# A Mamba block with SwiGLU on one core: GpSimd holds the product of beat 47, not of beat 48, behind the scan of beat 45

## The reference

```python
x_in, res = split(x @ W_in)                     # 512 + 512 columns
u = silu(causal_conv4(x_in))
dt, Bm, Cm = split(u @ W_x, [16, 32])
delta = softplus(dt @ W_dt + b_dt)
# 512 channels, 16 states each, a recurrence over the rows of a sequence:
h = exp(delta * A) * h + (delta * u) * Bm       # the scan
y = sum_over_states(h * Cm) + u * D
x = layernorm(x + (y * silu(res)) @ W_out)
x = layernorm(x + (silu(x @ Wg.T) * (x @ Wu.T)) @ Wd.T)
```

## Time and profile before

| | us |
|---|---|
| median of 3 runs | 1825.21 (1825.11 to 1825.59) |
| the profiled execution | 1827.21 |
| its span, first to last instruction | 1825.4 |
| PE busy | 1683.4 (92%) |
| DVE busy | 1711.8 (94%) |
| ACT busy | 1599.6 (88%) |
| POOL busy | 1646.8 (90%) |
| mean granted TensorE clock | 0.993 of full speed |

### The profile page before, as it was taken

The page is one execution under the profiler, slowest core; times in us unless marked ns, Lnnn a source line. Parts: engine busy times, 40 slices in busy tenths (PEclk is TensorE's granted clock), DMA queues, the critical chain, the costliest instruction groups (busy, mean ns, idle before and its releaser), DMA issues. The chain is left out here.

```text
span 1825.4 us, 32557 instructions
## 1 busy us (share of the span) xinstructions
PE 1683.4 (92%) x10128; PEld 1272.4 (70%) x10128; DVE 1711.8 (94%) x1958; ACT 1599.6 (88%) x2769; POOL 1646.8 (90%) x1629
## 2 busy tenths in 40 slices
PE   8879898999989899898999989899898999989788
PEld 3546686776767677676776767677676776767667
DVE  4999999999999999999999999999999999999994
ACT  4897989899898998989899898998989899898864
POOL 3999899998999999899998989999899998989970
PEclk9999999999999999999999999999999999999999
DMA  7323123222222323222232222323222232311010
GB/s 241 116 70 116 48 82 105 82 105 82 105 77 86 108 90 116 67 85 104 82 113 74 106 80 83 115 83 116 71 82 104 82 116 71 115 61 59 36 47 24
DMA packets 82108, 164.57 MB, mean 90 GB/s; under 512 B 10369, under 2 KB 28033, under 8 KB 81938
## 3 DMA queue, kind: packets, MB, share of 16 engines
q1 hardware_dynamic: 80498, 160.90, 25.6%
q10 hardware_dynamic: 1440, 1.58, 0.3%
HBM read 87.47 MB, written 8.91 MB: 53 GB/s over the span
## 5 line engine op out<-in xcount | busy, mean ns | idle before, releaser
L1236 POOL TENSOR_TENSOR dbu<-du,brep 128x512 f32<-128x512 f32 x1024 | 1315.1, 1314 | 120.6 <-DVE h L1431 97.0
L1431 DVE TENSOR_TENSOR_SCAN h<-da,carry,dbu 128x512 f32<-128x512 f32 x928 | 1151.6, 1271 | 54.7 <-ACT da L1093 42.5
L1093 ACT ACTIVATE da<-delta,a_s 128x512 f32<-128x512 f32 x928 | 641.6, 700 | 38.7 <-DVE h L1431 36.0
L1102 ACT ACTIVATE gt<-ht_upper,ct 128x512 f32<-128x512 f32 x512 | 353.3, 690 | 121.7 <-PE ht_upper L736 119.9
L736 PEld LDWEIGHTS ht_upper<-ident,h 128*128 128x128 f32 x2048 | 247.9, 141 | 215.8 <-issue 127.9
L736 PE MATMUL ht_upper<-ident,h 128*128 128x128 f32 x2048 | 311.7, 275 | 75.6 <-ACT gt L1102 46.3
L1443 DVE SCALAR_TENSOR_TENSOR acc<-ht_lower,ct,acc 128x512 f32<-128x512 f32 x480 | 349.3, 728 | 12.6 <-PE ht_lower L736 10.9
L736 PE MATMUL ht_lower<-ident,h 128*128 128x128 f32 x2048 | 312.9, 276 | 19.2 <-DVE acc L1443 16.7
L761 PE MATMUL y_upper<-ident,gt 128*128 128x128 f32 x2048 | 311.1, 275 | 0.0
L736 PEld LDWEIGHTS ht_lower<-ident,h 128*128 128x128 f32 x2048 | 240.2, 142 | 83.1 <-DVE h L1431 39.4
L761 PEld LDWEIGHTS y_upper<-ident,gt 128*128 128x128 f32 x2048 | 243.5, 142 | 56.0 <-issue 37.3
(11 more groups left out here) (189 smaller groups left out, 1909.6 us busy)
## 6 DMA issues: line engine op xcount, KB each, us to landing
brep<-b_rows SPq DMA_DIRECT2D x127, 512.0 KB, 3.7
xs<-xin SPq DMA_DIRECT2D x242, 256.0 KB, 2.5
xr<-x SPq DMA_DIRECT2D x16, 512.0 KB, 3.9
xt_s<-x_t SPq DMA_DIRECT2D x15, 512.0 KB, 3.8
out<-xr SPq DMA_DIRECT2D x15, 512.0 KB, 2.9
win_s<-w_in SPq DMA_DIRECT2D x2, 512.0 KB, 5.2
h<-xin SPq DMA_DIRECT2D x4, 256.0 KB, 4.3
h<-xin ACTq DMA_DIRECT2D x4, 256.0 KB, 4.7
```

The costliest lines, as they stand in the source:

```text
L1093: nc.scalar.activation(dst[:, :], delta[:, par, m, :], ACT.Exp, scale=a_s[:, m, n:n + 1])\
L1102: nc.scalar.activation(gt[:, (n * UPPER + k) % GT, :], ht_upper[:, :], ACT.Copy, scale=ct[:, par, k, n:n + 1])\
L1236: nc.gpsimd.tensor_tensor(dbu[:, beat % DBU, :], du[:, par, m, :], brep[:, n // PIECE % 2, n % PIECE, :], ALU.mult).then_inc(dbu_ready, 1)
L1431: nc.vector.tensor_tensor_scan(h[:, n % 2, m, 0:T], da[beat % 2][:, :] if slot is None else da_ahead[:, slot, :], dbu[:, beat % DBU, :], c ...
```

## The change

One number changes. HELD was {35: 33, 48: 45} and becomes {35: 33, 47: 45}. Product 47 now waits for scan 45 instead of scan 43. Product 48 waits for scan 44, as its buffer asks, which product 47's wait already includes. No instruction is added, removed or moved on any engine.

```diff
 AHEAD = 3
 DBU = 4
-HOLD = (4, 5)
+HOLD = (4, 4)
```

## The result

The changed kernel takes 1833.97 us (median of 5 runs, 1832.17 to 1835.08) against 1825.21 (1824.31 to 1825.59): a ratio of 1.0046, 95% interval 1.0031 to 1.0061. It is slower, by 8.8 us in the medians. The direction and the mechanism were forecast; the forecast was +5.8. The time lies above the 1829.0 to 1833.5 that the forecast had for itself, and inside the range of 1827.0 to 1834.0 by 0.03 us only.

What follows compares the result with a forecast made beforehand. GpSimd's gapless run from product 48 to the next chunk's product 0 was taken as the bound; +0.45 us in 11 middle chunks (4.95) plus the end chunks gave +5.8, 1825.2 to 1831.0 us, range 1827.0 to 1834.0.

Steps and rivals of the forecast that it cites:

- The bound: GpSimd, without idle time from product 48 to the next chunk's product 0, sets the loop of 109.14 us.
- The rival that VectorE sets the chunk: Each of 15 chunks would end 0.84 us earlier, -12.6, giving 1812.6 us; chance 0.07.
- The rival that scan 44 stays long: Scan 44 still held by something else, product 48 only delayed, 1.29 us in some 14 chunks: 1843 us; chance 0.04.
- The absorbed case: Delay mostly absorbed: product 48 only +0.22 us later per chunk, +2.4 in all, 1827.6 us; chance 0.14.
- The gain at scan 45: In a middle chunk scan 45 starts 0.84 us earlier, scan 44 being unstretched and up1's product waiting for its matmuls.
- The bound of 1.07: Largest gain at scan 45, 1.07 us, if the modelled end of up1's matmuls is too late; product 48 then +0.22.
- The delay: Product 47 and the copy precede product 48 after scan 45: 1.43 us against 0.15, so product 48 comes 1.29 later.
- The sum per loop: At product 48 in a middle chunk: -0.84 + 1.29 = +0.45 us, bounds +0.22 and +0.6.
- How it travels: Nothing absorbs +0.45 us from product 48 to the next chunk; scan 0 waits about 1.7, the whole loop is longer.
- The profiled executions: Whole program: the profiled execution would go from 1827.2 to 1833.0 us, +5.8.
- The clock rival: TensorE, waiting more near scan 3 of each chunk, drops to half speed for some work: about 1856 us; chance 0.03.
- The page's delay: Loser of the shared SBUF port starts some 115 ns after the winner's end; scan 44 would have ended at 983.6.

Runs made afterwards that it cites:

- the delay alone: Kernel before, with product 48 waiting for scan 46 instead of scan 45 and scan 44 still stretched by product 47: 1860.02 us, ratio 1.0188.
- no hold: Kernel before with HOLD (4, 0): nothing held at the second silus, product 48 waiting for scan 44 alone: 1825.48 us, ratio 1.0003.

## Why the prediction was right, and where it was short

**The bound.** Right, by both halves: a delay of product 48 by 2.43 us lengthened the loop by 2.43, and the removed 0.54 us of GpSimd work came back as 0.51 in the changed kernel and as 0.16 in the kernel before. The rival that VectorE sets the chunk is out: its part between scans 44 and 45 became 0.74 shorter and the time grew. The rival that scan 44 stays long is out by its row (1.27). The absorbed case is out by the loop, 0.55 longer where it had 0.22.

**The gain at scan 45.** I had 0.84; it is 0.74. The term is the start of up1's product. I let it follow its matmuls' recorded end by 0.04, the hand-over that `acc` showed; here it took 0.12 (matmuls end at 984.37, product at 984.49), and VectorE's products start a little less tightly when they don't stand as a pair. The bound of 1.07, which I kept for the low end, didn't come about.

**The delay.** I had 1.43 - 0.15 = 1.28 to 1.29, from the row of the first silus. It is 1.44 - 0.15 = 1.29.

**The sum per loop.** 0.55 (0.54 to 0.56) instead of 0.45, so the mis-sized term is the gain at scan 45. Over 11 middle chunks that is 6.0 instead of 5.0, about a third of the 3.0 us by which the forecast was too low (1834.0 against 1831.0). That the time still fell inside the range, 0.03 us from its end, is luck.

**How it travels.** Right in chunks 3 to 13: scan 0 waits 1.63 where I had 1.7, and the loop is 109.73 where I had 109.6. Of the ends: in the profiled executions the loop from scan 45 of chunk 14 to scan 45 of chunk 15 is 110.81 (110.70 in the second profile) against 109.56 before, +1.25, where 1.29 for the delay less 0.5 for chunk 15's scan 44 makes +0.79. The delay came as reckoned (+1.31 to scan 0) and scan 44 gave back 0.61; the rest, 0.55, is what chunk 15 lost from scan 0 to scan 44, and the difference is there from scans 5 to 6 on (2.43 us instead of 1.88). I had counted nothing for TensorE's clock there. Of the 10 us from 6 us after scan 0, the first row is the changed kernel, the second the kernel with the delay alone (columns PE, PEld, DVE, ACT, POOL, clock, DMA share, GB/s):

```profile
1684.50:1694.50 10.00, 9.92 (x60) 9.08 (x59) 8.23 (x9) 9.05 (x16) 9.54 (x10) 0.81 0.17 55
1713.97:1723.97 10.00, 9.46 (x65) 8.25 (x64) 8.98 (x9) 9.47 (x19) 10.00 (x10) 0.97 0.17 55
```

The kernel before has 0.97 there too. The lower clock goes with the lost 0.55, but the longer wait of TensorE behind scan 3 doesn't explain it: that stall grew from 2.77 to 3.98 us by the change, and it is as long with the delay alone, which kept 1.88 us from scan 5 to scan 6. What decides when the clock comes back stays open.

**The profiled executions.** They differ by only 5.0 us. The sum of the 15 loops grew by 6.6 (1639.5 to 1646.1), but chunk 0 was 1.7 shorter, from scan 0 to scan 45, in the profile after. That goes with the clock, not with the change: over the ten profiles of this study chunk 0 takes 74.7 to 74.8 us in four and 76.4 to 77.3 in six, the changed kernel once in each group, and the six have the longer stretch at half clock near 40 us. From 34 to 110 us, before and after:

```profile
34.00:110.00 76.00, 61.77 (x329) 38.28 (x327) 70.11 (x67) 61.68 (x94) 67.63 (x66) 0.93 0.31 108
```

```profile
34.00:110.00 76.00, 59.48 (x336) 37.85 (x335) 71.52 (x68) 63.09 (x96) 66.92 (x66) 0.98 0.31 108
```

In the second profile of the changed kernel, with a clock of 0.93 there, chunk 0 takes what it took before, the loops add up to 1646.8, and the span is 1832.8: +7.4 to a like execution. What is left to the 8.6 and 8.8 of the medians, some 1.3 us, stays open.

**The clock rival.** Wrong as I put it: TensorE's new stalls near scan 3 left the clock at 1.00 in chunks 8 and 9 (the two stretches above), as in the other middle chunks. In chunk 15 a lower clock goes with 0.55 us, between scans 5 and 6.

**The page's delay.** On the page "SBUF — State Buffer" of the Trainium skill, section "SBUF: two separate sides", the 115 ns stand for work of GpSimd that waits for VectorE's end, and I put them for either engine. The kernel before shows them in neither direction: 35 scans that met a product ended 1.08 to 1.09 us after the product's recorded end, and 30 products that met a scan ended 1.06 to 1.09 after the scan's, where either takes 1.27 alone. The one that waited resumed some 0.19 us before the other's recorded end, both ways.

## What to carry to other kernels

A hold that keeps two engines off a shared port has two ends: what the scan saves, and how many of the held engine's instructions then stand behind the release. Count the second to the point where the held engine is next waited for; if it has no idle time up to there, as here, each instruction put behind the release is paid in full. Holding each product only as long as its own conflict lasts (47 behind scan 44, 48 behind scan 45) kept the saving and paid nothing. A few microseconds at the two ends of the program can come and go with the phase of the engines or with the clock, whatever the change, so it's the loops in the middle that tell what a change of this size is worth. Before tuning such a place, cut a little work from the suspected engine, with and without the change: the two answers give the bound and the room to the next one.

## What the runs showed of the hardware that I had not expected

An engine that loses the port isn't only the scan or the product: the copy of 128x4 elements took 1.12 us beside scan 44 in the kernel before, and a normalisation of 256 columns 1.46 beside scan 45 with no hold, against 0.19 and 0.55 to 0.56 alone (the row of the kernel with no hold). How late the second starts decides what the meeting costs: 1.07 us when the product had just begun (scan 44 before, 1.26 of the product left), 0.14 when it was mostly through (scan 45 with no hold, 0.32 left). Both are what was left of the product, less 0.18 to 0.19. It holds for several products in a row: scan 43 of chunk 15 in the changed kernel takes 3.68 and ends 1.08 after the last of them.

Two executions of one kernel can differ by near 2 us in the first chunk alone: the same work took 76.7 us at a granted clock of 0.93 from 34 to 110 us, and 74.7 at 0.98.
